# Tokenizer of a ViT tower: pooled moments as four quarter products, and three engine orders shifted with them

## What is computed

```
x = features.reshape(b, c, h, s, w, s)                       # s = 4: patches of 4 x 4 = 16 pixels
reduce_feats = x.mean((3, 5)) ...                            # pooled tokens, [b, 256, 64]
q  = _ln(reduce_feats, ln_q_w, ln_q_b) @ Wq.T                # layer norm over the 64 channels
kv = _ln(unf, ln_kv_w, ln_kv_b) @ Wkv.T                      # the same for every pixel
attn  = softmax(einsum('bhpd,bhpnd->bhpn', q * scale, k))    # 8 heads, 16 pixels for each token
aggre = einsum('bhpn,bhpnd->bhpd', attn, v)
return reduce_feats + aggre @ proj_w.T + proj_b
```

## Time and profile before

| | |
|---|---|
| median of 3 runs | 650.3 us (649.91 to 650.62) |
| span of the profiled execution | 644.3 us |
| what lies around the span (median less span) | 6.0 us |
| TensorE matmul busy | 600.7 us, 93% of the span |
| VectorE busy | 538.7 us, 84% |
| ScalarE busy | 476.6 us, 74% |
| GpSimd busy | 473.0 us, 73% |

### The profile page before, as it was taken

The page is one execution under the profiler, slowest core; times in us unless marked ns, Lnnn a source line. Parts: engine busy times, 40 slices in busy tenths (PEclk is TensorE's granted clock), DMA queues, the critical chain, the costliest instruction groups (busy, mean ns, idle before and its releaser), DMA issues.

```text
span 644.3 us, 16919 instructions
## 1 busy us (share of the span) xinstructions
PE 600.7 (93%) x5362; PEld 325.9 (51%) x5362; DVE 538.7 (84%) x1027; ACT 476.6 (74%) x942; POOL 473.0 (73%) x453
## 2 busy tenths in 40 slices
PE   3999999999999999998779989998689999999995
PEld 1222333333333333332345656665378889898894
DVE  4589999999999999998747888998887888888882
ACT  3888777777778777873358878887568878888882
POOL 5957988889988898755850456666787877777777
PEclk9999999999999999999869999999989999999998
DMA  8432233333322233000029492111131222222210
GB/s 287 156 145 97 112 131 132 132 131 131 116 76 88 115 132 132 20 2 14 1 78 200 98 211 54 39 37 38 56 102 53 68 66 72 60 53 67 57 40 1
DMA packets 49755, 58.04 MB, mean 90 GB/s; under 512 B 32476, under 2 KB 45252, under 8 KB 47448
## 3 DMA queue, kind: packets, MB, share of 16 engines
q1 hardware_dynamic: 44280, 48.12, 25.2%
q0 software_dynamic: 5120, 6.99, 3.5%
q10 hardware_dynamic: 288, 2.10, 0.9%
HBM read 50.13 MB, written 10.28 MB: 94 GB/s over the span
## 4 chain that ended last, share of the span: by engine, by line
PE 39%; DVE 6%; issue 2%; POOL 1%; DMA 1%; ACT 1%; POOLq 0%; DVEq 0%; ACTq 0%
PE s_logits L2078 13%; PE s_delta L2051 3%; PE s_proj L2051 3%; DVE x_px L1484 2%; PE s_ln L2085 2%; PE s_proj L1663 2%; PE s_logits L1757 2%; PE s_delta L1685 2%; PE s_ln L2056 2%; PE s_proj L2056 2%; PE s_proj L1673 1%; PE s_proj L1698 1%; PE s_proj L1697 1%; PE s_ln L1644 1%; PE s_ln L1735 1%
## 5 line engine op out<-in xcount | busy, mean ns | idle before, releaser
L2103 POOL DMA_INDIRECT out<-orow,m_rows x96 | 119.1, 1241 | 34.6 <-issue 19.1
L815 PE MATMUL s_proj<-x_px,w_kv 64*64 64x512 f32 x256 | 129.9, 599 | 0.0
L812 PE MATMUL s_proj<-x_px,w_kv 64*64 64x512 f32 x256 | 129.1, 596 | 0.4 <-DVE vec L235 0.3
L1205 POOL DMA_INDIRECT rows_by_group<-r_pay,r_slot_i x64 | 68.5, 1070 | 44.9 <-DVE r_slot_i L1534 8.4
L486 POOL TENSOR_TENSOR half_px<-x_px 128x1024 f32<-128x1024 f32 x30 | 71.4, 2380 | 32.9 <-DMA x_px<-in_x 32.9
L507 POOL TENSOR_TENSOR pre<-va 128x1024 f32<-128x1024 f32 x32 | 76.2, 2380 | 22.5 <-DVE va L608 20.7
L1947 DVE TENSOR_TENSOR m_xs<-m_rows,m_path_w 128x768 f32<-128x768 f32 x96 | 91.3, 951 | 1.1 <-PE s_proj L2056 0.7
L592 DVE TENSOR_TENSOR qk<-s_proj,q 128x512 f32<-128x512 f32 x128 | 85.5, 679 | 7.4 <-PE s_proj L815 5.1
L2078 PE MATMUL s_logits<-m_xsT,m_w_cur 128*64 128x128 f32 x1152 | 83.3, 275 | 0.0
L608 DVE TENSOR_TENSOR va<-b_a,v_sb 128x1024 f32<-128x1024 f32 x62 | 75.6, 1220 | 7.5 <-PE b_a L837 7.5
L308 ACT ACTIVATE x_sq<-x_px 128x1024 f32<-128x1024 f32 x64 | 67.1, 1048 | 19.2 <-PE b_x L872 19.2
(11 more groups left out here) (320 smaller groups left out, 1781.1 us busy)
## 6 DMA issues: line engine op xcount, KB each, us to landing
x_px<-in_x SPq DMA_DIRECT2D x15, 2048.0 KB, 7.9
m_rows<-rows_by_group SPq DMA_DIRECT2D x96, 72.0 KB, 1.9
wt<-in_w2T SPq DMA_DIRECT2D x8, 512.0 KB
rows_by_group<-rows_by_group SPq DMA_DIRECT2D x1, 2286.0 KB, 9.6
x_px<-in_x ACTq DMA_DIRECT2D x2, 1024.0 KB, 6.4
out<-orow,m_rows POOLq DMA_INDIRECT x96, 2.7
rows_by_group<-r_pay,r_slot_i POOLq DMA_INDIRECT x64
wt<-in_w2T SPq DMA_DIRECT2D x2, 256.0 KB
```

Of the source, the lines that this page charges most:

```text
L812: mm(b_k[i][LO, :], w_kv[LO, 0, LO], px(t, j, LO), start=True, stop=True)
L815: mm(b_k[i][HI, :], w_kv[HI, 0, HI], px(t, j, HI), start=True, stop=True).then_inc(done["kv_product"], 1)
L1205: g.indirect_dma_start(rows_d, bass.IndirectOffsetOnAxis(ap=slot_i[:, c % 2, k:k + 1], axis=0), pay[:, c % 2, k, :], None).then_inc(scatte ...
L2103: nc.gpsimd.indirect_dma_start(out_d, bass.IndirectOffsetOnAxis(ap=rows[:, i, ID0:ID0 + 1].bitcast(I32), axis=0), orow[:, i, :], None, bou ...
```

## The change

`q_moments` becomes four products of 256 columns, one on each quarter of the array, and goes to the two banks of `b_a` in place of `b_x`. For that the squares of the two images are written with their halves swapped (two instructions of 64 partitions in place of one of 128). Since `b_a` is now shared, `q_moments` waits for the last `va_mul`, and `spread(t-2, 0)` waits for `q_var(t)`. The orders of TensorE, ScalarE and VectorE are moved along: `q_moments` goes up behind `kv(t-1, 5)`, all spreads go to later places in the round, and `va_mul` with them.

```diff
         def pool_square(t):
...
-            a.activation(rs2[:, TOK:2 * TOK], rs2[:, 0:TOK], ACT.Square, scale=NP ** -0.5).then_inc(done["pooled_squared"], 1)
+            for at, of in ((LO, HI), (HI, LO)):
+                a.activation(rs2[at, TOK:2 * TOK], rs2[of, 0:TOK], ACT.Square, scale=NP ** -0.5).then_inc(done["pooled_squared"], 1)
...
         for t in range(TILES + 2):
             kv_ln(t - 2)
+            copy_v(t - 2, 7)
+            kv_rstd(t - 2)
             q_ln(t - 1)
-            kv_rstd(t - 2)
-            copy_v(t - 2, 7)
+            copy_v(t - 1, 0)
             q_rstd(t - 1)
-            copy_v(t - 1, 0)
+            square(t - 1, 1)
             q_final(t - 1)
+            copy_v(t - 1, 1)
+            softmax_exp(t - 2)
+            kv_mean(t - 1)
             square(t - 1, 2)
-            softmax_exp(t - 2)
-            copy_v(t - 1, 1)
-            kv_mean(t - 1)
             copy_v(t - 1, 2)
...
             square(t, 0)
             pool_square(t)
-            square(t, 1)
+            kv_clamp(t - 1)
             copy_v(t - 1, 5)
-            kv_clamp(t - 1)
+            q_mean(t)
             copy_v(t - 1, 6)
-            q_mean(t)
...
             qk_mul(t - 2, 5)
+            q_var(t - 1)
+            qk_mul(t - 2, 6)
+            qk_mul(t - 2, 7)
             va_mul(t - 3, 0)
-            qk_mul(t - 2, 6)
-            q_var(t - 1)
-            qk_mul(t - 2, 7)
+            scale_scores(t - 2)
+            scores_max(t - 2)
+            q_scale(t - 1)
             va_mul(t - 3, 1)
-            scale_scores(t - 2)
-            q_scale(t - 1)
-            scores_max(t - 2)
-            va_mul(t - 3, 2)
             shift_scores(t - 2)
             qk_mul(t - 1, 0)
             qk_mul(t - 1, 1)
+            va_mul(t - 3, 2)
             sum_exps(t - 2)
...
         def spread(t, i):
...
             if i == 0:
                 pe.wait_ge(done["weights"], 2 * t + 2)
+                if t + 2 < TILES:
+                    pe.wait_ge(done["q_var"], t + 3)
...
         def q_moments(t):
...
-            pe.wait_ge(done["pooled_squared"], t + 1)
+            pe.wait_ge(done["pooled_squared"], 2 * t + 2)
...
+            if t > 2:
+                pe.wait_ge(done["va_ready"], 4 * (t - 2))
+            mm(b_a[LO, 0, 0:TOK], avg_px[LO, LO], rs2[LO, 0:TOK], start=True, stop=True)
+            mm(b_a[HI, 1, 0:TOK], avg_px[LO, LO], rs2[LO, TOK:2 * TOK], start=True, stop=True)
+            mm(b_a[LO, 1, 0:TOK], avg_px[HI, HI], rs2[HI, TOK:2 * TOK], start=True, stop=True)
+            mm(b_a[HI, 0, 0:TOK], avg_px[HI, HI], rs2[HI, 0:TOK], start=True, stop=True).then_inc(done["q_moments"], 1)
...
-            mm(b_x[LO, :], avg_px[LO, LO], rs2[LO, :], start=True, stop=True)
-            mm(b_x[HI, :], avg_px[HI, HI], rs2[HI, :], start=True, stop=True).then_inc(done["q_moments"], 1)
...
         for t in range(TILES + 4):
             kv(t - 1, 1)
             mean(t - 1)
+            if t < TILES + 2:
+                spread(t - 3, 2)
             kv(t - 1, 2)
...
+            kv(t - 1, 3)
             spread(t - 3, 3)
-            kv(t - 1, 3)
...
             kv(t - 1, 5)
...
-            spread(t - 2, 0)
-            kv(t - 1, 6)
             q_moments(t)
...
+            kv(t - 1, 6)
             kv(t - 1, 7)
+            spread(t - 2, 0)
+            kv(t, 0)
+            scores(t - 1, 1)
             spread(t - 2, 1)
...
-            kv(t, 0)
-            scores(t - 1, 1)
             q_mm(t)
-            spread(t - 2, 2)
+            if t == TILES + 1:
+                spread(t - 2, 2)
```

More of the change, by code:

```diff
@@ L333, in q_mean @@
                 act.wait_ge(done["q_scaled"], t)
-            a.activation(rq[:, :], b_x[:, 0:TOK], ACT.Square).then_inc(done["q_mean_sq"], 1)
+            a.activation(rq[:, :], b_a[:, 0, 0:TOK], ACT.Square).then_inc(done["q_mean_sq"], 1)
         def q_ln(t):
@@ L577, in pool_last @@
             v.wait_ge(done["pooled_biased"], t)
-            v.wait_ge(done["pooled_squared"], t)
+            v.wait_ge(done["pooled_squared"], 2 * t)
             v.wait_ge(done["q_product"], t)
@@ L684, in q_var @@
             v.wait_ge(done["q_mean_sq"], t + 1)
-            d.scalar_tensor_tensor(rq[:, :], rq[:, :], -1.0, b_x[:, TOK:2 * TOK], ALU.mult, ALU.add).then_inc(done["q_var"], 1)
+            d.scalar_tensor_tensor(rq[:, :], rq[:, :], -1.0, b_a[:, 1, 0:TOK], ALU.mult, ALU.add).then_inc(done["q_var"], 1)
         def q_scale(t):
@@ L878, in q_moments @@
                 return
-            pe.wait_ge(done["pooled_squared"], t + 1)
+            pe.wait_ge(done["pooled_squared"], 2 * t + 2)
             if t == 0:
                 pe.wait_ge(folded, 1)
-            if t > 0:
-                pe.wait_ge(done["kv_var"], t)
-            mm(b_x[LO, :], avg_px[LO, LO], rs2[LO, :], start=True, stop=True)
-            mm(b_x[HI, :], avg_px[HI, HI], rs2[HI, :], start=True, stop=True).then_inc(done["q_moments"], 1)
+            if t > 2:
[4 more added lines that the diff above has]
+            mm(b_a[HI, 0, 0:TOK], avg_px[HI, HI], rs2[HI, 0:TOK], start=True, stop=True).then_inc(done["q_moments"], 1)
         def q_mm(t):
@@ L891, in q_mm @@
             pe.wait_ge(done["q_var"], t + 1)
+            if t > 0:
+                pe.wait_ge(done["kv_var"], t)
             mm(b_x[LO, 0:TOK], gq[LO, LO], rs2[LO, 0:TOK], start=True, stop=True)
```

## The result

| | before | after |
|---|---|---|
| median | 650.46 us (649.91 to 651.64, 4 runs) | 660.75 us (658.06 to 663.59, 4 runs) |
| ratio, 95% interval | | 1.0176 (1.0146 to 1.0207) |
| span of the profiled execution | 644.3 us | 657.7 us (its own time 659.9) |
| round in the middle of the tokenizer | 18.15 us | 19.00 us |

The forecast was 657.6 us and slower. The direction and the place of the loss were right, and the median lies inside the range; the size was 3 us short. Part A, from scores to `square_sum`, is 10.94 us (10.95 forecast). Part B is 8.06 us (7.74 forecast).

A forecast was written before the change was run, and what follows sets the result against it. TensorE bounds the tokenizer, VectorE having nothing to spare at `square_sum`. Parts A + 21.8, parts B - 13.7, early rounds - 0.8 make + 7.3 us: span 651.6, plus 6.0 around it, 657.6 us; range 651.5 to about 661.

The forecast's parts named there:

- Bound and place: TensorE sets the tokenizer's pace; VectorE's `finish` reaches `square_sum` together with TensorE, so VectorE has nothing to spare there.
- Part A, 10.95: From `scores(t-1, 1)` to `square_sum`: grows from 9.27 to 10.95 us, with TensorE standing still 0.82 us at `square_sum`.
- The walk: VectorE's starts stepped through new part A: `q_scale` at c + 2.61, `va_mul 2` 6.37, `finish` 10.44, ending 10.86.
- Four products together: At `q_moments`, four products of 256 columns run together on the quarters, taking 0.43 us instead of 0.86.
- the rival in which they go in pairs: `q_moments` doesn't run its four products together: + 6.5 us, 664; 5%, shared with `q_scale` making `mean` late.
- Part B, 7.74: From `square_sum` to the next scores: 7.59 us plus 0.15 waiting for pooled squares at `q_moments`, 1.14 less than before.
- The upper bound that I kept for it: Pooled squares ahead of `q_moments`: second one 0.40 us behind the first, + 0.09 x 15 = 1.4 us at the high end.
- The sum: Whole tokenizer: + 21.8 for 13 parts A, - 13.7 for 12 parts B, - 0.8 for early rounds; together + 7.3 us.
- The three rounds ahead: Early rounds without `finish` at `square_sum`: each saves 0.43 us less a 0.15 wait, together - 0.8 us.
- The start and the tail: Tail behind the last `square_sum`: taken as 0, bounds - 1.1 and + 0.4 us; the sum has no term for the start.
- the 6.0 around it: Time outside the span: 6.0 us added to the forecast span of 651.6 to give 657.6 us.
- Its lower end: Low end 651.5 us, the no-change case: wait at `q_scale` but none at `va_mul 2`, part A 10.48; 7%.

The follow-up runs named there:

- the kernel with `weigh` ahead: Changed kernel with ScalarE's order mended, `out_mm` ahead of spread 3, and `finish`, `recip`, `qk_mul` 3, `weigh` ahead of `va_mul` 3: 1.0014 of the kernel before.
- the same, two products: Kernel with `weigh` ahead, but pooled moments as before: one square of 128 partitions, two products of 512 columns into `b_x`; 1.0207 of the kernel before.
- the repeat: The changed kernel unaltered, run again on another chip: 659.22 us against 648.48 for the kernel before, ratio 1.0176.
- the kernel with the pooled squares first: Changed kernel with ScalarE squaring the pooled tokens ahead of the first part of the next tile's pixels: 1.0236 of the kernel before.
- The kernel before with late finish: Kernel before, with VectorE's `finish` moved behind `recip` and the next `qk_mul`: single times, 680.0 us against 670.5 for the kernel before.

## Why the forecast was right, and where it was not

**Bound and place.** Right. VectorE had nothing in hand at `square_sum`; moving `finish` by 0.81 us in the kernel before cost 0.81 a round. `finish` is the releaser in every row of `square_sum` in the changed kernel.

**Part A, 10.95.** Measured 10.94. The walk was right to 0.06 us at each step but one: `scores_max` starts 0.73 us and not 0.62 behind `scale_scores`, whose result it reads (in the earlier trace rows `q_scale` stood between the two). That costs nothing, since `q_scale` waits for `q_mm` anyway. Two small errors offset: `va_mul 2` and with it `finish` came 0.06 us early, and `square_sum` follows 0.56 us behind the start of `finish` and not 0.51. That 10.94 met 10.95 to a hundredth is partly luck. The stop takes 0.91 us and not 0.82, since part A without one is 10.03 (the kernel with `weigh` ahead) and not 10.13.

**Four products together.** Right. The records on the four quarters start at 157.18 to 157.20 and follow one another by 0.27 and 0.21 us, and the rival in which they go in pairs fell. The Trainium skill, TensorEngine Tiling (Array Packing), Restrictions and Gotchas, has it that different row tiles can't write one PSUM bank together; in these rows they do (157.18 to 157.20), where their outputs lie on different partitions.

**Part B, 7.74: the failed step.** "The second of the two follows about 0.31 us behind the first (0.40 less the 0.09 by which such operations overlap)". That gave the pair 0.71 us; it takes 0.85, so the second is about 0.43 behind (0.85 less one of 0.42), and the pair doesn't overlap with the square ahead of it either. Counted from `square_sum`'s start, the pair was forecast to begin at 3.01 and end at 3.72 us; it began at 3.13 and ended at 3.98. `q_moments` is ready at 3.62, as forecast, and starts at 4.03: a wait of 0.41 in place of 0.15. The upper bound that I kept for it (the second 0.40 behind the first) is near for the pair, but left out the 0.12 us ahead of it. The rest of the 0.32 us by which part B missed is that it takes 7.70 us without waits, 0.11 above my 7.59; of the 0.41 us of wait, 0.36 show in part B (8.06 less 7.70). Part A without waits came out 0.10 below, so TensorE alone is 17.73 us a round, against 17.72 in the forecast. The round is 0.31 us over the forecast: 0.26 are the later squares, 0.09 the longer stop at `square_sum`, and 0.05 go off again at `q_moments`.

**The sum.** By the measured parts: 13 x 1.67 - 12 x 0.82 = + 11.9 us, where I had 21.8 - 13.7 = + 8.1. That is the 3.8 us by which the forecast was short in the steady rounds, and all of it is part B. Two terms beside it had the wrong sign or size:
- The three rounds ahead, "- 0.8". This was a slip, too: by my own parts the part B of tile 2 already has the full - 1.14, so the sum should have had - 0.28 - 0.28 - 1.14 = - 1.7. Measured from the first `square_sum` (22.63 and 24.16) to tile 2's scores (63.87 and 66.23) it is + 0.83 us. The view names five stops of TensorE in this stretch after, and none before: 0.24 us at `q_moments` twice (pooled squares), 0.44 at `mean` (`q_scale`, which has 0.26 us to spare only in a full round), 0.33 at a `kv` chunk (`copy_v`), and 0.34 at the scores behind tile 1's `weigh` (this round has no stop at `square_sum` ahead of it):

```profile
28.20 0.43 PE L887 MATMUL b_a<-rs,avg_px 64*64 64x256 f32 x1 [0.24 <-ACT rs L319]
34.68 1.92 PE L862 MATMUL b_x<-x_px,msel 128*32 128x512 f32 x16 [0.44 <-DVE qs L696]
38.87 0.61 PE L813 MATMUL s_proj<-x_px,w_kv 64*64 64x512 f32 x1 [0.33 <-ACT v_sb L401]
43.93 0.43 PE L887 MATMUL b_a<-rs,avg_px 64*64 64x256 f32 x1 [0.24 <-ACT rs L319]
60.02 1.07 PE L850 MATMUL b_s<-qk,sel 128*32 128x512 f32 x8 [0.34 <-DVE a_sb L679]
```

These sum to 1.59 us, but a figure in brackets leaves out what the record ahead runs on behind its 0.43 us, and the shortest stops have none. Counted from when the quarter is free, the five are 0.42, 0.51, 0.51, 0.42 and 0.52 us (at `mean` and the scores less the gap that the kernel before has there), and three more `kv` chunks are late by 0.32 (30.72), 0.14 (56.74) and 0.21 us (63.49): 3.05 us after. In the kernel before two chunks are late too, by 0.25 (35.31) and 0.09 us (36.28). TensorE's work in the stretch is 2.15 us less (three times 0.43 and one spread). - 2.15 + 3.05 - 0.34 = + 0.56; the 0.27 left to + 0.83 are about the 0.05 us by which the first product behind each of these stops is longer (the last section). So the term was wrong in its waits: it had 0.15 us three times, and they are 3.05 in all.

- The start and the tail, taken as 0. The start is + 1.5 in the profiled executions, 0.4 of it the order. The tail, from the last `square_sum` on, is 13.4 - 14.1 = - 0.7, inside my bounds. Up to the last `finish` it is 32.08 against 33.69 us, - 1.6, and from there on + 0.9. But the clock differs there: a spread of the last tile has records of 1.01 to 1.06 us before (from 308.25 on) and of 0.59 after (from 322.73 on). So neither can be put to the order. The stretches of the tokenizer's end, before and after, show it in the column behind GpSimd's:

```profile
291.00:318.00 27.00, 22.20 (x152) 7.87 (x151) 20.89 (x37) 10.25 (x19) 18.96 (x13) 0.94 0.03 9
318.00:350.00 32.00, 26.27 (x129) 15.10 (x128) 18.84 (x31) 20.00 (x42) 11.99 (x27) 0.84 0.54 124
350.00:644.00 294.00, 272.39 (x2711) 213.00 (x2708) 246.37 (x563) 226.66 (x516) 204.87 (x232) 0.98 0.28 66
```

```profile
305.00:331.00 26.00, 21.13 (x151) 7.28 (x152) 21.28 (x37) 9.66 (x18) 18.79 (x13) 1.00 0.04 9
331.00:363.00 32.00, 26.48 (x136) 15.18 (x135) 19.68 (x33) 21.32 (x46) 12.39 (x27) 0.89 0.47 121
363.00:657.00 294.00, 272.90 (x2703) 213.10 (x2701) 245.08 (x561) 226.03 (x513) 202.91 (x232) 0.98 0.28 66
```

The stages behind the tokenizer are unchanged in the program, as forecast; from the last `finish` to the end they take 319.6 and 320.5 us. All terms together give the spans: 11.9 + 0.8 + 1.5 - 0.7 = 13.5, against 657.7 - 644.3 = 13.4.

**Span and median.** I added "the 6.0 around it". In all four runs of the changed kernel 2.2 us lie around the span, and in the kernel before on the other chips as well. If that holds for its profiled execution, this took about 646.5 us and was a quick one, 3.8 us under the median. Its early rise of the clock may be one cause; the only other profiled execution with such a start, that of "the same, two products", is the quickest of its five too (657.73 against a median of 662.05). The medians differ by 10.3 us and, in the repeat, by 10.7, less than the spans. So the number came out nearer than its terms, by luck: the forecast difference of spans was 7.3 and the real one 13.4, while the forecast of the median missed by 3.

**The range.** Its upper end was 661.0 us, and the median 660.75. That it holds is luck too: the terms that were off (the early rounds, part B) are larger than the margin that I gave them. Its lower end had a small slip: part A without the wait at `va_mul 2` is 10.95 - 0.43 = 10.52 and not 10.48, which gives 652.0 and not 651.5 and changes no reading.

## What to carry to other kernels

When a change moves a block of work from one side of a hand-over to the other, walk the engine on the other side to the hand-over first: where both arrive together, what the block delays it by is paid in full, every round. When one instruction is split in two small ones, count the whole duration for each, and look for what stood close behind them. A shorter round isn't yet a shorter kernel: count how often each part of it is paid, and read the first rounds for themselves.

## What the runs showed of the hardware beyond that

- Two ScalarE activations on 64 partitions with 256 columns take 0.84 to 0.85 us together, twice the time of one on 128 partitions with the same columns (0.40): half the partitions save nothing. Where input and output lie on different halves, the first of them also starts 0.03 us behind the end of the instruction ahead instead of 0.10 ahead of it.
- On VectorE the reduction `scores_max`, right behind `scale_scores` whose result it reads, starts 0.73 us after it. With `q_scale` between the two they are 0.96 us apart, of which `q_scale` takes 0.34 (156.39 to 156.73): 0.62 without it.
- The first product on a quarter after a stop of TensorE or after products of 32 columns takes longer by some hundredths: four `q_moments` take 0.48 us behind the stop (157.18 to 157.66), and 0.43 without one (158.10 to 158.53 in the kernel with the pooled squares first).
- From the first product of `kv 0` on, TensorE's records have the length of 1.2 GHz for none of the time or for over 3.5 us, in two executions with the same instructions up to there, and the first `square_sum` comes 2.3 us later. The granted clock reads 1.00 in that stretch; only the records' durations (1.06 for 0.59) show it. The kernel before with late finish, in the view of stretches:

```profile
15.00:19.00 4.00, 3.66 (x20) 1.62 (x21) 0.91 (x3) 1.70 (x4) 2.19 (x1) 1.00 1.00 430
```
